# Experts put behind the head attention in one program, with seven of the eight expert fronts inside its last steps

## The reference

```python
x = x + _L0_attn_ref(_layernorm(x), ...)     # 16 heads of 8
x = x + _L0_xattn_ref(_layernorm(x), ctx_1024, ctx_1024, ...)
x = x + _L0_ffn_ref(_layernorm(x), ...)      # shared expert + top 2 of 8, 256 wide, sigmoid router
x = x + _L1_attn_ref(_layernorm(x), ...)     # grouped, relative position bias
x = x + _L1_xattn_ref(_layernorm(x), ctx_1024, ctx_1024, mask, ...)
x = x + _L1_ffn_ref(_layernorm(x), ...)      # top 2 of 8, 128 wide, softmax router, gated shared expert
```

## Time and profile before

| | before |
|---|---|
| median of 3 runs | 1279.44 us |
| the profiled execution, its span | 1277.92 us, 1276.1 us |
| busy in the span: TensorE, VectorE, ScalarE, GpSimd | 90%, 75%, 59%, 54% |
| mean granted TensorE clock | 0.933 |
| TensorE's granted clock, 40 slices (9 is nearly full, 5 half) | 9599999999977999999999899997799999858998 |

### The profile page before, as it was taken

The page is one execution under the profiler, slowest core; times in us unless marked ns, Lnnn a source line. Parts: engine busy times, 40 slices in busy tenths (PEclk is TensorE's granted clock), DMA queues, the critical chain, the costliest instruction groups (busy, mean ns, idle before and its releaser), DMA issues. The chain is left out here.

```text
span 1276.1 us, 33899 instructions
## 1 busy us (share of the span) xinstructions
PE 1145.8 (90%) x10468; PEld 806.3 (63%) x10468; DVE 959.5 (75%) x2103; ACT 757.1 (59%) x1729; POOL 693.2 (54%) x967
## 2 busy tenths in 40 slices
PE   3799989999967999999999798888999999668997
PEld 2466656666556777777777576665455555466775
DVE  5588899888944878788878677775677777437996
ACT  1377787777744555555555377664356565436775
POOL 8667798667642556665666501117656562224554
PEclk9599999999977999999999899997799999858998
DMA  5765688666402011111010100003554542005441
GB/s 149 161 143 117 143 174 174 145 130 132 100 11 101 39 67 67 67 68 50 16 66 1 44 6 1 0 1 73 113 120 99 113 99 66 2 24 215 190 191 49
DMA packets 49454, 112.56 MB, mean 88 GB/s; under 512 B 11873, under 2 KB 31617, under 8 KB 47281
## 3 DMA queue, kind: packets, MB, share of 16 engines
q1 hardware_dynamic: 38816, 86.80, 26.9%
q0 software_dynamic: 5376, 18.88, 4.9%
q10 hardware_dynamic: 5136, 5.31, 2.0%
HBM read 88.09 MB, written 22.02 MB: 86 GB/s over the span
## 5 line engine op out<-in xcount | busy, mean ns | idle before, releaser
L1442 POOL TENSOR_TENSOR experts_shared_out<-experts_act_out,experts_share 128x512 f32<-128x512 f32 x136 | 188.7, 1388 | 134.9 <-ACT experts_act_out L1607 111.0
L1613 ACT CAST experts_hidden_hi<-experts_hidden 128x512 fp32r<-128x512 f32 x216 | 134.1, 621 | 112.7 <-DVE experts_hidden L1530 77.2
L1549 DVE TENSOR_TENSOR experts_hidden_lo<-experts_hidden,experts_hidden_hi 128x512 fp32r<-128x512 f32 x184 | 197.3, 1072 | 0.9 <-ACT experts_hidden_hi L1613 0.8
L712 DVE TENSOR_REDUCE heads_neg_max<-heads_ps_max 128x4 f32<-128x512 f32 x256 | 168.9, 680 | 34.3 <-PE heads_ps_max L889 32.6
L1607 ACT ACTIVATE experts_act_out<-experts_ps_gate 128x512 f32<-128x512 f32 x216 | 128.6, 596 | 69.3 <-PE experts_ps_gate L1661 67.2
L777 ACT ACTIVATE heads_E<-heads_ps_exp 128x512 f32<-128x512 f32 x256 | 149.9, 603 | 21.3 <-PE heads_ps_pv L911 16.5
L1530 DVE TENSOR_TENSOR experts_hidden<-experts_shared_out,experts_ps_up 128x512 f32<-128x512 f32 x136 | 92.0, 676 | 65.9 <-POOL experts_shared_out L1442 52.4
L712 DVE TENSOR_REDUCE cross_neg_max<-cross_ps_max 128x4 f32<-128x512 f32 x128 | 86.9, 686 | 48.1 <-PE cross_ps_max L889 47.5
L1659 PE MATMUL experts_ps_y<-experts_hidden_hi,experts_down_hi 128*128 128x512 f32 x216 | 94.8, 439 | 21.9 <-DVE experts_hidden_lo L1549 12.6
L889 PE MATMUL heads_ps_max<-QK 48*128 48x128 bf16 x1024 | 102.4, 225 | 9.8 <-DMA QK<-heads_qk_parts 5.2
L265 POOL TENSOR_TENSOR norm_var_eps<-norm_moments,norm_eps 128x2 f32<-128x2 f32 (+1 forms) x72 | 22.2, 308 | 162.4 <-DVE norm_moments L258 162.4
(11 more groups left out here) (232 smaller groups left out, 2967.8 us busy)
## 6 DMA issues: line engine op xcount, KB each, us to landing
experts_share<-experts_cT_dram SPq DMA_DIRECT2D x7, 2304.0 KB, 8.5
experts_share<-experts_cT_dram SPq DMA_DIRECT2D x7, 2048.0 KB, 7.2
heads_qk_parts<-heads_parts POOLq DMA_DIRECT2D x32, 384.0 KB, 4.5
QK<-heads_qk_parts SPq DMA_DIRECT2D x64, 192.0 KB
QK<-heads_qk_parts SPq DMA_DIRECT2D x64, 128.0 KB
cross_qk_parts<-cross_parts POOLq DMA_DIRECT2D x16, 384.0 KB, 3.8
QK<-cross_qk_parts SPq DMA_DIRECT2D x32, 192.0 KB
QK<-heads_qk_parts SPq DMA_DIRECT2D x64, 64.0 KB
```

Of the source, the lines that this page charges most:

```text
L712: nc.vector.tensor_reduce(neg_max[:, half, heads.start:heads.stop], ps_max[:, u % 2, :].rearrange("q (h k) -> q h k", h=HU), AX.X, ALU.max ...
L1442: nc.gpsimd.tensor_tensor(as_group(shared_out[c % 2][:]), as_group(act_out[b][:]), share[t.k % 2][:, row, :, :], ALU.mult).then_inc(weight ...
L1549: nc.vector.tensor_tensor(hidden_lo[b][:], hidden[b][:], hidden_hi[b][:].bitcast(F32), ALU.subtract).then_inc(lo_dve, 1)
L1613: nc.scalar.copy(hidden_hi[b][:], hidden[b][:]).then_inc(hi_ready, 1)
```

## The change

`experts` no longer opens a block. It returns a `Follow`, a set of functions that write its instructions into the lists of the block of `head_attention`, so that the barrier and the clearing of semaphores between attention and experts fall away. In the attention's last seven steps each engine writes fronts behind its step's own work: `FRONTS` gives the turns for each step, from NB_ALL - 4 to NB_ALL + 2, and turns 7 and 8 follow the last step. The rest of the experts part is as before. To make room, the expert tiles are allocated where the attention's tiles and the staging tiles were (`tiles.close()`, `staging.close()` before `make_follow`), and `ps_tok` and `ps_y` lie on the banks of `ps_max` and `ps_xv`, whose last use is in step NB_ALL - 4. Before the first front that writes there, ScalarE waits for all cut pieces, the folds and one DMA, and TensorE for the last maxima. So the splitting has to end earlier: LATE_SPLIT is now WORK + 10 (step 30 in `heads0`, 22 in `cross1`), the folds go to steps 52 to 55, and in `cross1` the hardware loop covers steps 4 to 11 only (8 more steps are written out) and WORK is 12 instead of 20. The three small loads of the router are issued at the attention's start.

```diff
+        tiles = ExitStack()
-            return ctx.enter_context(nc.sbuf_tensor(f"{name}_{label}", shape, dt))
+            return tiles.enter_context(nc.sbuf_tensor(f"{name}_{label}", shape, dt))
...
-        LOOPS = [(i * B + 4, i * B + 20) for i in range(NL)]
-        WORK, LATE_SPLIT, BULK = LOOPS[0][1], NB_ALL - 4, (-4, 4)
+        LOOPS = [(i * B + 4, i * B + (20 if NL > 1 else 12)) for i in range(NL)]
+        WORK, BULK = LOOPS[0][1], (-4, 4)
+        LATE_SPLIT, FOLDS = WORK + 10, NB_ALL - 12
+        FRONTS = {NB_ALL - 4: (-1,), NB_ALL - 3: (0,), NB_ALL - 2: (1,), NB_ALL - 1: (2,), NB_ALL: (3, 4), NB_ALL + 1: (5,), NB_ALL + 2: (6,)}
+        LAST_FRONTS = (7, 8)
...
+        tiles.close()
+        staging.close()
+        follow = make_follow(ctx, normed, over)
...
+            follow.sp_start(sp)
...
+                if t.reg is None:
+                    if t.k == NB_ALL - 3:
+                        act.wait_ge(prep_lo, SPLIT_PIECES + Prepare.PIECES)
+                        need(act, prep_fold, 3 * len(prepare.folds))
+                        if prepare.by_rel is not None:
+                            act.wait_ge(by_rel_stored, 16)
+                    for j in FRONTS.get(t.k, ()):
+                        follow.act_front(act, Turn(None, j))
             joined_steps(act, lead, lead and lead.act, emit, FIRST, LOOPS, LAST)
+            for j in LAST_FRONTS:
+                follow.act_front(act, Turn(None, j))
+            follow.act(act)
...
+                    if t.k == NB_ALL - 3:
+                        pe.wait_ge(max_taken, UNITS * NB_ALL)
+                        pe.wait_ge(v_ready, NG_ALL)
+                    for j in FRONTS.get(t.k, ()):
+                        follow.pe_front(pe, Turn(None, j))
```

796 lines of the change are left out of this document (414 added, 382 removed).

## The result

The changed kernel takes 1261.79 us (median of 4 runs, 1259.05 to 1262.95), the kernel before beside it 1279.62 us. The ratio is 0.9864, 95% interval 0.984 to 0.9888. Seven more executions of the changed kernel came later, at 1260.23 to 1272.04 us; over all eleven the median is 1262.95.

What follows compares the result with a forecast made beforehand. TensorE paces attention's last steps, then runs the fronts at clock 0.50 at both attention-to-experts junctions. 1277.9 - 11.2 - 11.7 (junctions) + 2.5 (cuts) = 1257.5; the median lies 1.5 us above the profiled execution, so 1259 us, range 1250 to 1268.

Steps and rivals of the forecast that it cites:

- the prediction's own case: Behind attention's last transposition the clock falls to 0.50 after fronts 3 and 4; 11.2 and 11.7 us saved; chance 0.42.
- A front's price in a full step: Steps 61 to 63: TensorE pays each front in full at full clock, 0.6, 1.5 and 1.5 us, 3.6 together.
- From T on: From the end of attention's last transposition (T) to the first routing instruction: 11.7 us at full clock, 13.9 with the fall.
- Its closing list: Expected profile: first routing instruction some 16 to 18 us after attention's last transposition, plus 3.6 us of longer steps.
- holding through: Rival: clock stays full through all fronts behind attention; 4.4 us better, 1254.6 us; chance 0.24.
- The earlier fall: Rival: clock falls one step earlier, before turn 3; 2.9 us worse in each layer, 1264.8 us; chance 0.20.
- rival "slower": Clock falls inside steps 61 to 63 already; 19.4 us a layer lost against 13.4 saved, 1294 us; chance 0.04.
- signs of being wrong: Front steps growing much over 1.5 us, ScalarE idling in step 61, or experts' first group later relative to first routing instruction.
- Steps swallow more: Rival: TensorE waits for ScalarE, steps 61 to 63 each grow 1.1 us more, 31 to 35 too; 1268 to 1276; chance 0.07.
- The cuts: Down-matrix cuts moved into steps 31 to 34 of `heads0` delay GpSimd's splits, which everything follows: +2.5 us, between 0.9 and 2.9.
- What stands behind L1480: After the first routing instruction, the routing chain and the weights' trip through DRAM were taken as unchanged, at no cost.
- `cross1`'s cuts and written-out steps at nothing: In `cross1` earlier cuts hide beside fully busy TensorE, and eight written-out loop steps cost nothing.

Runs made afterwards that it cites:

- after_timed: The changed kernel, unaltered, timed in more rounds and profiled again: median 1264.52 us over 6 runs, ratio 0.9892.
- after_again: The changed kernel, unaltered, in a second profiled execution: 1272.04 us.

## Why the prediction came out

The forecast was 1259 us with 1250 to 1268, the median 1261.79; the time is in the range. At five of the six junctions in the three traces of the changed kernel the clock fell behind turns 3 and 4, as in the prediction's own case, though about a turn later, at T + 5.1 to T + 7.7. By its steps:

- *A front's price in a full step*, 0.6 and twice 1.5 us, 3.6 a layer: step 60 to T grew by 2.9 us in `heads0` and step 28 to T by 3.0 in `cross1` wherever the clock was full, by 0.45, 1.22 and 1.25 us for the three turns. Right, a little dear.
- *From T on*, with the clock falling behind turns 3 and 4, T + 13.9: measured T + 13.0 and T + 13.7 (fall at T + 5.1 and T + 6.5), T + 12.7 and T + 12.6 in `after_timed` (fall at T + 6.4 and T + 7.7). The order of the chain (difference of turn 5, norm, normalisation, last turns) is what the rows show. What the prediction lacked in it is the last normalisation's second price: 1.1 us as it had it, but 2.0 to 3.0 us beside a difference of GpSimd, and this makes most of the step from T + 12.6 to T + 13.7: in `cross1` of `after_timed` and of `after_again` the clock fell at T + 7.7 both times, and the routing came at the one and at the other. Its closing list asked for 16 to 18 us behind T plus 3.6, which does not follow from its own T + 13.9; only with the 3.6 inside does it fit, and then 13.0 + 2.9 = 15.9 and 13.7 + 3.0 = 16.7 were measured. The saving was 12.8 + 12.4 us, not 11.2 + 11.7.
- *The clock's rivals*: holding through gives T + 11.7 by the prediction; with the clock full to T + 9.8, and the norm already ahead, it was T + 10.8. The earlier fall exists too. In one of three executions of the changed kernel it came inside step 63 of `heads0`, the mechanism of my rival "slower", and there steps 63 and 64 did grow by 3.1 and 3.6 us instead of 1.5, one of the signs of being wrong that I had named. Behind T that rival was right: it had 5.1 us more than T + 11.7, so T + 16.8, and T + 16.3 was measured. In the steps it was mis-sized: I gave it 14.3 us more and measured were 4.3 (step 60 to T 23.8 instead of 19.5), since only the rest of step 63 and step 64 ran at 0.50. It came in one layer only, so the total was 1272 and not 1294.
- *Steps swallow more* by ScalarE's wait: no, the steps grew by less than the fronts' own time.
- *The cuts*, +2.5: 1.9 us without a 0.50 stretch, 3.1 to 3.3 with one, 8.0 with two, and 3.5 in the one trace that has no stretch and a longer step 31. Between 0.4 and 0.9 us came back in steps 37 to 52 of the changed kernel's three traces. The mechanism was right; the clock on top of it, and what comes back, were missing.
- *The folds*, no term of the sum: steps 52 to 60, in which they lay before too, grew by 0.8 to 1.7 us. Their place four steps earlier is the only edit there; it was not tried alone.
- *What stands behind L1480 "is left as it is"*: this is the step that failed. The table load cost 1.3 us, the boundary with the clearing behind `experts0` 2.0, the groups 1.8, the end of the program 0.8, and these come in every execution of the changed kernel: 5.9 us that the sum had at nothing. The first group lost 0.5 to 1.4 us more. The prediction had named a later first group relative to L1480 as a sign of being wrong, and the sign came, in layer 0.
- *`cross1`'s cuts and written-out steps at nothing*: steps 2 to 28 became 1.2 us shorter. Which of the edits did this is not tried.

That the sum came so near is in part luck. For the profiled pair it forecast 20.4 us less and 17.1 was measured. Against the forecast 11.5 us were lost: 6.6 behind L1480 as above (0.6 of it in the first group), 0.8 in steps 52 to 60, 0.8 at the cuts, and 3.3 between `shared1` and step 2 of `cross1`, where the two traces of the kernel before differ by 2.6 themselves. And 8.1 us were won that the forecast had not: 2.3 at the junctions, 3.0 in the opening, which is no effect of the change, 1.1 in steps 2 to 28 of `cross1`, 1.2 in the groups of `experts1`, which took 96.3 us in another execution as before the change, and 0.5 elsewhere. Against the eleven runs (1262.95) the forecast is 4 us too low.

## What to carry to other kernels

Work moved from a gap into full steps gains more than the gap's idle time where the clock is down in the gap: here a front costs 1.2 us in the steps and 2.5 behind them. Whether the fuller steps also bring the fall of the clock forward is open: it fell early in three of nine executions with them and in none of five without. When two parts are merged into one block, look at what the boundary did besides: where the semaphores are cleared now, and how many waits stand ahead of an activation that needs another table. A norm moved forward by 2 us gained between nothing and 2 us, by what its normalisation then ran beside. And take more than one trace before a few us are given a cause: one program had its routing at 381.3 and at 392.1 us.

## What the runs showed of the hardware

- The same program got its 0.50 stretches at different places in each execution, and its times lay between 1259.0 and 1272.0 us. Of the 11 us between two profiled executions 7.5 lay at one junction. The kernel before, in many more executions, stayed within 1274.6 to 1282.2.
- A table load that is given waits of its own starts only after them: 1.28 us moved from under a wait into the chain. In the changed kernel no drain shows behind it: the load ends at 383.58 and the sigmoid starts at 383.59.
- With TensorE busy 12.28 of 13.40 us behind T, added products of 512 columns among it, the clock stayed at 1.00; with 21.16 of 21.30 us of fronts, after it had fallen, it stayed at 0.50. The busy share of a profile did not tell the level, as the prediction's rows had shown for the fronts.
- VectorE's four normalisations of 128x128 took 1.11 us alone and 2.05 us when a difference of 128x512 on GpSimd began with them (1.26 us); beside two of these they took 3.00 us. The differences themselves took 1.26 to 1.29 us. Over all fourteen traces no single normalisation that ran without a difference beside it took over 0.38 us, while 47 of the 147 that overlapped one took 0.9 us or more.
- Eight products of the router (128x16) took 0.96 us at clock 1.00 and 1.73 us at 0.50; the prediction's bound from the weight loads had been 0.87.
